# Two heads in the two row halves of the matrix unit, and experts' token rows gathered 128 at a time

## The reference

```python
x = x + L0_attn(layernorm(x));  x = x + L0_ffn(layernorm(x))
x = x + L1_attn(layernorm(x));  x = x + L1_ffn(layernorm(x))
...
# L0 attention, per batch and head (d = 16, S = 1024)
scores = where(causal, rope(q) @ rope(k).T / 4, -max);  z = softmax(scores) @ v
...
# L1 ffn: 6 experts a token out of 3 of 8 groups; an expert has C = 96 slots
slot = expert * C + minimum(position_in_expert, C - 1)
buf[slot] = x[token]                      # 64 x 96 rows of 256
out = (silu(buf @ Wg.T) * (buf @ Wu.T)) @ Wd.T
y = sum_k out[slot_k] * weight_k + shared(x)
```

## Time and profile before

| | us |
|---|---|
| median of 3 runs (1574.81 to 1579.88) | 1579.84 |
| the profiled execution | 1579.99 |
| its span, first to last instruction | 1578.3 |
| PE busy | 1407.0 |
| DVE busy | 1050.9 |
| ACT busy | 813.1 |
| POOL busy | 375.3 |

### The profile page before, as it was taken

One profiled execution on the slowest core, in us unless ns is written; L12 is line 12 of the kernel. 1 busy time (PEld: TensorE's weight loads), 2 busy tenths in 40 slices (PEclk: granted clock), 3 DMA queues, 4 the chain that ended last, 5 costly groups with the idle time before them and its releaser, 6 DMA issues. The chain is left out here.

```text
span 1578.3 us, 36418 instructions
## 1 busy us (share of the span) xinstructions
PE 1407.0 (89%) x12869; PEld 985.8 (62%) x12869; DVE 1050.9 (67%) x2197; ACT 813.1 (52%) x1676; POOL 375.3 (24%) x796
## 2 busy tenths in 40 slices
PE   3848999998669999999979999999998798699977
PEld 2414555454555777777767677777777645599953
DVE  4766777775766888888841888888882368522229
ACT  1215656556216777777730787777781115333330
POOL 0344656430020111111120111111101000477730
PEclk9968999999869999999999999999999789799985
DMA  3027999972023755556540566556652340599948
GB/s 100 1 59 158 243 250 240 212 170 54 1 77 77 139 134 137 133 136 139 136 91 1 112 138 140 135 133 140 140 122 44 106 118 0 141 290 300 283 131 291
DMA packets 463402, 215.08 MB, mean 136 GB/s; under 512 B 412083, under 2 KB 434449, under 8 KB 463073
## 3 DMA queue, kind: packets, MB, share of 16 engines
q1 hardware_dynamic: 448992, 175.09, 46.9%
q0 software_dynamic: 12000, 36.90, 7.9%
q10 hardware_dynamic: 2336, 2.16, 0.4%
HBM read 81.97 MB, written 31.52 MB: 72 GB/s over the span
## 5 line engine op out<-in xcount | busy, mean ns | idle before, releaser
L1055 PE MATMUL bank<-a_pt,v_part 128*128 128x128 f16 x3456 | 234.2, 219 | 14.9 <-DMA a_pt<-a_ph 9.5
L737 DVE TENSOR_REDUCE a_qh<-bank 128x1 f16<-128x1024 f32 (+7 forms) x256 | 182.3, 755 | 86.5 <-PE bank L627 84.9
L1118 ACT ACTIVATE a_ph<-a_p,a_rinv 128x1024 f16<-128x1024 f32 (+7 forms) x256 | 198.6, 777 | 79.0 <-POOL a_rinv L997 76.0
L1055 PEld LDWEIGHTS bank<-a_pt,v_part 128*128 128x128 f16 x3456 | 207.7, 98 | 48.4 <-DMA a_pt<-a_ph 7.8
L1126 DVE TENSOR_REDUCE a_negm<-bank 128x1 f32<-128x1024 f32 (+7 forms) x256 | 191.8, 750 | 55.9 <-PE bank L1039 55.7
L1034 PE MATMUL bank<-a_k,a_q 128*128 128x512 f16 (+3 forms) x1152 | 228.6, 326 | 0.2
L725 ACT ACTIVATE a_p<-bank 128x1024 f32<-128x1024 f32 (+7 forms) x256 | 158.0, 650 | 129.8 <-PE bank L682 113.8
L1160 DVE SCALAR_TENSOR_TENSOR a_ph<-a_p,a_rinv,a_ph 128x1024 f16<-128x1024 f32 (+7 forms) x256 | 206.9, 808 | 1.7 <-ACT a_ph L1118 1.7
L1107 ACT ACTIVATE a_p<-bank,a_negm 128x1024 f32<-128x1024 f32 (+7 forms) x256 | 189.5, 740 | 21.6 <-DVE a_negm L1126 21.5
L997 POOL TENSOR_TENSOR a_rinv<-a_rinv,p_scale 128x1 f32<-128x1 f32 x256 | 49.0, 191 | 615.4 <-DVE a_rinv L1139 615.2
L906 PE MATMUL bank<-x_part,wsplit 128*128 128x512 f16 x768 | 187.3, 381 | 4.0 <-PEq L188 1.8
(11 more groups left out here) (206 smaller groups left out, 2246.4 us busy)
## 6 DMA issues: line engine op xcount, KB each, us to landing
wgu<-in_wgu SPq DMA_DIRECT2D x64, 352.0 KB
choice_rows<-zero POOLq DMA_DIRECT2D x24, 512.0 KB, 5.2
c_rows<-choice_rows SPq DMA_DIRECT2D x16, 768.0 KB, 11.5
wsplit<-w_parts POOLq DMA_DIRECT2D x30, 384.0 KB, 3.9
wd<-in_wd SPq DMA_DIRECT2D x64, 176.0 KB
pw_in<-in_wqkv SPq DMA_DIRECT2D x16, 384.0 KB, 5.3
w_parts<-pw_part SPq DMA_DIRECT2D x16, 384.0 KB, 2.9
a_pt<-a_ph SPq DMA_TRANSPOSE x256, 3.0
```

Source lines behind the costliest of these rows:

```text
L737: dve.tensor_reduce(qh[s][:, i, MC:MC + 1], s1_place(t), AX.X, ALU.max, negate=True).then_inc(m_ready, 1)
L1055: ins = eng.matmul(Z_ps[:, cols], g.vs[par][v_][:, k, :], turned[slot][:, a * blocks[j] + k, :], start=(k == 0 and (v_, a) == PARTS[0]), s ...
L1118: eng.activation(parts[slot][:, 0:w_], probs[slot][:, 0:w_], ACT.Copy, scale=rinv[:, p_, jj:jj + 1]).then_inc(p_hi, 1)
```

## The change

In the first attention the unit of work is a pair of heads. A head's 48 used columns (high and low parts of queries against high and low of keys, three products instead of four) fit in 64, so one row of 128 holds both heads, and one DMA transposition turns both. A head's matmuls then use 64 rows of the array, the pair's other head the other 64. Row scores and column scores are cut to pieces of at most 512 columns, 24 a pair (`ROWS`, `COLS`), and each step issues a column piece of one head and a row piece, equally wide, of the other. The masks are two matmuls of 64 rows. There are three buffers for row scores and three for column scores. Rows with more than 512 keys have their maximum taken in two pieces and then joined. Rows run 13 of 24 steps ahead. Keys are turned twice, once for rows, once for columns; the queries are copied twice. The order in the two queues is by pairs, with two pieces of weights each.

In the experts the 384 slots of four experts are gathered as three times 128 rows; the token numbers are brought into this order by six matmuls with a shifted identity (a new constant). The first three groups are gathered before the loop, the weights of experts 10 to 15 only after the first group's rows are turned. Four experts' rows are turned at a time, by six transposes of 128 rows. The overflow weights are turned after the loop. Two constants are loaded in addition: 128 KB before x, 108 KB in the last norm.

```diff
+    ROWS = ((6, 1), (6, 0), (4, 1), (5, 0), (5, 1), (7, 1), (2, 0), (7, 0), (0, 0), (3, 0), (1, 0), (4, 0))
+    COLS = ((0, 0), (7, 0), (0, 1), (6, 0), (1, 0), (5, 0), (2, 0), (3, 1), (3, 0), (2, 1), (4, 0), (1, 1))
+    NC_ = len(ROWS)
+    NS = 2 * NC_
+    NB_ = 3
+    EARLY = 13
...
+        ST = [g.bank[0][:, 0, :], g.bank[0][:, 1, :], g.bank[1][:, 0, :]]
+        S1 = [g.bank[2][:, 0, :], g.bank[2][:, 1, :], g.bank[1][:, 1, :]]
...
+        def row_piece(t):
+            i, c4 = ROWS[(t + 1) // 2 % NC_]
+            return t % 2, i, 4 * c4, min(4, i + 1 - 4 * c4)
+        def col_piece(k):
+            kb, c4 = COLS[k // 2]
+            return k % 2, kb, kb + 4 * c4, min(4, BT - kb - 4 * c4)
...
+        def halves(h):
+            at = slice(h * HP, (h + 1) * HP)
+            pairs = ((g.identb[at, :], g.maskb[at, :]), (g.swapped[at, 0, :], g.swapped[at, 1, :]))
+            return pairs if h == 0 else pairs[::-1]
...
+                def queries(dst, m, done):
+                    q = dst[m % 2].rearrange("p t (h c) -> p h t c", h=2)
+                    src = g.qk[:, 2 * m:2 * m + 2, :, 0, :]
+                    pool.tensor_copy(q[:, :, :, 0:2 * DH0], src).then_inc(done, 1)
+                    pool.tensor_copy(q[:, :, :, 2 * DH0:MC], src[:, :, :, 0:DH0]).then_inc(done, 1)
...
                 def fetch(m):
                     if m >= 2:
-                        pool.wait_ge(t_in[m % 2], 32 * (m // 2))
-                    if m >= 4:
-                        pool.wait_ge(tm_in[m % 2], 16 * (m // 2 - 1))
-                    q, k, done = qh[m % 4], kh[m % 2], w_in[m % 2]
-                    for a in range(2):
-                        src = g.qk[:, m:m + 1, :, 0, :].rearrange("p o t d -> p (o t) d")
-                        pool.tensor_copy(q[:, :, a * 2 * DH0:(a + 1) * 2 * DH0], src).then_inc(done, 1)
-                        src = g.qk[:, m:m + 1, :, 1, a * DH0:(a + 1) * DH0].rearrange("p o t d -> p (o t) d")
-                        dst = k[:, :, a * 2 * DH0:(a + 1) * 2 * DH0].rearrange("p t (r d) -> p t r d", r=2)
-                        pool.tensor_copy(dst, src.unsqueeze(2).to_broadcast([P, BT, 2, DH0])).then_inc(done, 1)
-                    pool.memset(q[:, :, MC:MC + 1], 0.0).then_inc(done, 1)
+                        pool.wait_ge(t_in, 32 * (m - 1))
+                        pool.wait_ge(tb_in, 16 * (m - 1))
+                    queries(qh, m, w_in)
+                    k = kh[m % 2].rearrange("p t (h c) -> p h t c", h=2)
+                    src = g.qk[:, 2 * m:2 * m + 2, :, 1, :]
+                    pool.tensor_copy(k[:, :, :, 0:DH0], src[:, :, :, 0:DH0]).then_inc(w_in, 1)
+                    pool.tensor_copy(k[:, :, :, DH0:MC], src).then_inc(w_in, 1)
...
+                def fetch_again(m):
+                    if m >= 2:
+                        pool.wait_ge(tm_in, 16 * (m - 1))
+                    queries(qhm, m, wm_in)
...
-                    if m >= 2:
-                        fetch_values(m - 2)
+                    fetch_again(m)
                 w_begin(pool)
-                for m in range(4, NH):
+                for m in range(2, NP):
                     fetch(m)
+                    fetch_again(m)
                     fetch_values(m - 2)
-                    if m - 4 < WJOBS:
-                        w_split(pool, m - 4)
-                    if m - 4 < ZD:
-                        pool.dma_start(zv[m - 4], g.zero[:, :]).then_inc(g.s_zero, 16)
-                for m in (NH - 2, NH - 1):
-                    fetch_values(m)
+                    for q in (2 * m - 4, 2 * m - 3):
+                        if q < WJOBS:
+                            w_split(pool, q)
+                        if q < ZD:
+                            pool.dma_start(zv[q], g.zero[:, :]).then_inc(g.s_zero, 16)
+                fetch_values(NP - 2)
+                fetch_values(NP - 1)
...
+                def turned(dst, src, m, done):
+                    sp.dma_start_transpose(dst[m % 2].rearrange("p (t n) -> p t n", n=P),
+                                           src[m % 2].rearrange("p t d -> p (t d)")).then_inc(done, 16)
                 def turn(m):
-                    sp.wait_ge(w_in[m % 2], FETCH * (m // 2 + 1))
+                    sp.wait_ge(w_in, FETCH * (m + 1))
+                    if m >= 1:
+                        sp.wait_ge(t_in, 32 * m)
                     if m >= 2:
-                        sp.wait_ge(s1_ready, (m - 1) * BT)
-                    sp.dma_start_transpose(qT[m % 2][:, :, :], qh[m % 4].rearrange("p t d -> p (t d)")
-                                           ).then_inc(t_in[m % 2], 16)
-                    if m >= 4:
-                        sp.wait_ge(st_ready, (m - 3) * BT)
-                    sp.dma_start_transpose(kT[m % 4][:, :, :], kh[m % 2].rearrange("p t d -> p (t d)")
-                                           ).then_inc(t_in[m % 2], 16)
+                        sp.wait_ge(s1_ready, (m - 1) * NS)
+                    turned(kT, kh, m, t_in)
+                    turned(qT, qh, m, t_in)
+                def turn_keys(m):
+                    if m >= 1:
+                        sp.wait_ge(tb_in, 16 * m)
+                    if m >= 2:
+                        sp.wait_ge(st_ready, (m - 1) * NS)
+                    turned(kTb, kh, m, tb_in)
...
                 turn(0)
                 turn(1)
+                turn_keys(0)
                 w_load(sp, 0)
                 w_load(sp, 1)
-                for m in range(NH):
-                    sp.wait_ge(m_ready, (m + 1) * BT)
+                for m in range(NP):
+                    sp.wait_ge(c_ready, 2 * m + 2)
+                    if m >= 1:
+                        sp.wait_ge(tm_in, 16 * m)
                     if m >= 2:
-                        sp.wait_ge(st_ready, (m - 1) * BT)
-                    sp.dma_start_transpose(qmT[m % 2][:, :, :], qh[m % 4].rearrange("p t d -> p (t d)")
-                                           ).then_inc(tm_in[m % 2], 16)
-                    if m + 2 < NH:
+                        sp.wait_ge(st_ready, (m - 1) * NS)
+                    turned(qmT, qhm, m, tm_in)
+                    if m + 2 < NP:
                         turn(m + 2)
-                    if 0 <= m - 3 < WJOBS:
-                        w_store(sp, m - 3)
-                        if m - 1 < WJOBS:
-                            w_load(sp, m - 1)
+                    for q in (2 * m - 2, 2 * m - 1):
+                        if 0 <= q < WJOBS:
+                            w_store(sp, q)
+                    for q in (2 * m, 2 * m + 1):
+                        if 2 <= q < WJOBS:
+                            w_load(sp, q)
+                    if m + 1 < NP:
+                        turn_keys(m + 1)
...
+                def scores(col, row):
+                    if col is not None:
+                        k, m, par, at_start = col
+                        hc, kb, q0, nc_ = col_piece(k)
+                        if k == 0:
+                            pe.wait_ge(tm_in, m * 16 + 16)
+                            pe.wait_ge(tb_in, m * 16 + 16)
+                        if not (at_start and k < NB_):
+                            pe.wait_ge(e_ready, m * NS + (k - NB_ + 1))
+                        at = slice(hc * HP, (hc + 1) * HP)
+                        cs = ST[k % NB_]
+                        c_diag = q0 == kb
+                        ci = pe.matmul(cs[:, 0:nc_ * P], kTb[par][at, kb * P:(kb + 1) * P],
+                                       qmT[par][at, q0 * P:(q0 + nc_) * P], start=True, stop=not c_diag)
+                    if row is not None:
+                        t, m, par, at_start = row
+                        hr, i, k0, nr_ = row_piece(t)
+                        if t == 0:
+                            pe.wait_ge(t_in, m * 32 + 32)
+                        if not (at_start and t < NB_):
+                            pe.wait_ge(m_ready, m * NS + (t - NB_ + 1))
+                        at = slice(hr * HP, (hr + 1) * HP)
+                        rs = S1[t % NB_]
+                        r_diag = k0 + nr_ == i + 1
+                        ri = pe.matmul(rs[:, 0:nr_ * P], qT[par][at, i * P:(i + 1) * P],
+                                       kT[par][at, k0 * P:(k0 + nr_) * P], start=True, stop=not r_diag)
+                    for x in range(2):
+                        if col is not None and c_diag:
+                            ident, mask = halves(hc)[x]
+                            ci = pe.matmul(cs[:, x * HP:(x + 1) * HP], mask, ident[:, x * HP:(x + 1) * HP],
+                                           start=False, stop=x == 1)
+                        if row is not None and r_diag:
+                            ident, mask = halves(hr)[x]
+                            ri = pe.matmul(rs[:, (nr_ - 1) * P + x * HP:nr_ * P], ident, mask[:, x * HP:P],
+                                           start=False, stop=x == 1)
+                    if col is not None:
+                        ci.then_inc(st_ready, 1)
```

(71 more changed lines are left out.)

## The result

| kernel | median us (runs) | ratio to before, 95% interval |
|---|---|---|
| before | 1580.33 (1574.81 to 1583.76, 6) | |
| changed | 1569.06 (1561.55 to 1572.1, 6) | 0.9921 [0.9893, 0.995] |

The changed kernel is 11.3 us faster, 8 us less than forecast. Its profiled execution is its slowest run: 1572.1 us, span 1570.0, mean granted clock 0.924.

A forecast was written before the change was run, and what follows sets the result against it. In the first attention the chain of GpSimd, SyncE and weight loads was to lead at 18.7 us a round, above the free pace of 14.5. Sum: 1579.99 - 13.2 (attention) - 6.3 (experts) + 0.4 (start) = 1561 us, range 1552 to 1571.

The forecast's parts named there:

- The chain leads: First attention: GpSimd's fetches and splits with SyncE's transposes, stores and weight loads set the pace, 18.7 us a round.
- The output-weight rounds: First attention, last eight weight pieces: no scaling and a shorter subtraction make the chain's round 16.1 us.
- fetch(3): First attention, early: GpSimd's copies for pair 3 done at 132 us.
- fetch(14): First attention, late: GpSimd's copies for pair 14 done at 327.3 us, after which the free pace holds.
- The free pace: First attention: a pair that waits for nothing else takes 14.5 us (13.5 to 15.5).
- The rival of the clock: First attention: waits for keys lower TensorE's clock; at 1.2 GHz throughout 1630 us; chance 0.06 for most of the attention.
- its mild form: Half-speed steps after each wait hide behind the chain and cost 3 to 8 us in the last pairs: 1567.
- The halves: First attention, TensorE: scores in opposite row halves run side by side, 12.1 to 13.9 us a pair.
- The rival of halves one after the other: First attention: row halves don't overlap, TensorE takes 18.1 us a pair, total 1591; chance 0.13.
- The experts: Start of the experts: loop starts at 1367.3 for 1374, 6.5 us gained (3.6 to 8); 6.3 in the sum.
- packing: Start of the experts: putting the token indices in the new order makes the last gather 0.4 us late.
- The overflow: End of the experts: its chain ends some 7.5 us after the last expert starts, hidden behind VectorE's 10.79 us wait.

The follow-up runs named there:

- e8: e1 with VectorE's division of a pair's output spread between the maxima of five steps instead of one block; 1537.2 us.
- e12: e8 with SyncE's stores of the split weights also moved ahead of the turning of a later pair; 1539.1 us.
- e6: e1 with the row piece and column piece of a step in the same half of the array's rows; 1575.7 us.
- e11: The changed kernel with VectorE's output division in parts, as in e8, and SyncE's loads left behind the turning; 1559.5 us.
- e10: e1 with four useless small TensorE matmuls added at step 0 of each pair but the first; 1546.2 us.
- e4: The changed kernel with the row piece and column piece of a step in the same half of the array's rows; 1576.7 us.
- e3: The kernel before with the attention's part of the change alone; 1572.6 us.
- e1: The changed kernel with SyncE's loads of a pair's weight pieces moved ahead of the turning of a later pair; 1560.6 us.

## Why the prediction was partly right

- **The chain leads.** Right in kind: the round is the one I wrote down, GpSimd waits 7 us a round for loads, and moving the loads ends it. Its sum was 18.7 and is 17.7: the load takes 4.5 (I took 5.2), the rest of the difference is 0.15 on stores, 0.1 on the copies. The output-weight rounds take 14.0 to 15.1, not 16.1. They are still the chain, for GpSimd waits in them as before:
```profile
280.95 0.61 POOL L893 CAST pw_part<-pw_in 128x512 f16<-128x512 f32 x1 [7.00 <-DMA pw_in<-in_wo]
```
The round from 272.74 is 2.66 of transposes, 1.15 of stores, 4.40 to GpSimd's start, 4.77 of splits and 1.86 of copies, 14.84. But the pairs themselves take 14.9 to 16.6 by then, so it no longer holds them up. fetch(3) came at 132.7, forecast 132; fetch(14) at 316.2, forecast 327.3. Here the kernel was 11 us ahead of the forecast.
- **The free pace** is the step that failed: "a pair that waits for nothing else takes 14.5 us". The last six turnings of queries are 14.9 to 16.6 apart, and from 316.2 to the attention's end it took 73.4 us, forecast 57.9. The size was right for a pair without gaps (14.07 in e8 and e12), and the terms too: halves overlap (e6), VectorE at 12.8 a pair by e12's row for 13.3. Missing were two things: VectorE's block before a maximum, 0.9 a pair, and the clock, 1.5 in each pair with a fall. In e11, where the keys come as in the changed kernel to within 2.2 us and the block is cut up, the same stretch takes 61.0. So the 11.1 us in hand and 4.4 more were lost, and the gain was 8.4 instead of 13.2 (the end before was 398.0, not the 398.4 of the forecast).
- **Luck.** That the attention's end is off by only 4.4 us is two errors that cancel: the chain 11.1 too slow, the part behind it 15.5 too quick. The profiled 1572.1 is 11.1 above 1561: 4.8 from the attention, nothing from the experts, 5.3 and 1.1 from the two rows of the table for which no cause is shown. The median, 1569.1, is within the range by 2 us.
- **The rival of the clock** I had given 0.06 for a clock low through most of the attention; its mild form, 1567, had no chance of its own and lay within the forecast's range. It is what happened: falls of 3.4 us, median 1569.1. I put the falls on waits for keys and took them for covered by the chain. In the middle they were: e11's rounds are as long as the changed kernel's. At the end, where no wait for keys was left, they came from a wait that I had not looked for. The kernel before has VectorE's block too, but at 240.67, just ahead of the value session at 241.19, and none of TensorE's waits from 236 to 256 us is over 0.25 us; the clock was 0.99. That its slack is what kept the clock up is my reading; no run took the slack away alone. The page that I cited is borne out, by e10 more than by the profile: the Trainium skill (TensorE: Matmul & The Clock Gate, "HAM oscillation") tells of waits in every round that bring the clock down again and again. Its waits are for DMA, some 3 to 5 us each; here 0.70 and 1.06 us for VectorE stood ahead of falls.
- **The halves**: right. The rival of halves one after the other is out, and its own price (1591) was too high: e4, the changed kernel without the overlap, takes 1576.7.
- **The experts**: right in sum, 6.3 for 6.3, with two terms off. The first turning starts at once behind the shared matmuls, but those start later: from the last pick's end to the first addition it is 3.8 us, before 2.2, so packing costs 1.6 there, not 0.4. From the pick's end to the first turning that leaves 1.9 gained, forecast 3.5. From the turning to the product 0.3 are lost, forecast 0.5; the first expert's product takes 1.4 for 2.8, as forecast; and the overflow's turning gone from there gives 3.4, forecast 3.0. The pick's end also came 2.4 earlier behind the router's table load, 95.3 us for 97.6, but that is no gain of the change: kernels with the same code there take 95.2 to 100.6. The loop takes 146.8 us to the last product, before 146.7, as forecast. The overflow stays hidden, behind 9.29 us.
- **From VectorE's first product to the end** 1.1 us more, forecast 0. The eleven other kernels with the new experts' part take 203.2 to 205.0 us from there, before and e3 203.3 and 202.0: about a microsecond, left open.

## What to carry to other kernels

When a change takes work off the engine that leads, gaps that this engine had time to absorb can become waits. Here a wait of a microsecond was followed by 3.4 us at half clock, and the pair took 1.5 us longer: look for blocks on the other engines that stand between two instructions it waits for, and cut them up. Where a chain through a slow queue and a limit of the engines lie close together, test both remedies together: here each alone brought 8.5 to 10 us and both 32. Put a load ahead of whatever in its queue waits for the engine that will use it; here that alone ended the attention 8.5 us earlier. And before you put a gain down to one part of a change, look which engine's wait ends last at that place: about half of the 8.0 us at the start of the experts came from moving ScalarE's copies away, not from rows that came sooner.

## What was not expected of the hardware

- Useless matmuls (1.05 us a pair) made the attention of e1 end 9.0 us sooner: the granted clock stayed at 1.00 from 140 to 340 us instead of 0.93.
- In the changed kernel 0.70 us of waiting (200.71) stood ahead of a fall, in e1 1.06 (312.01); in e1 a fall cost a pair 1.5 us.
- Two score matmuls of 64 rows in opposite halves, 512 columns each, took 0.28 us together with their masks, and one of 128 rows before 0.23 by itself.
